# Last stage of a mixture-of-experts kernel in chunks of neighbouring tokens, with the residual added in the expert tiles

## What is computed

```python
gate_logits = jnp.einsum('bpd,de->bpe', x, W_gate)
top_w, top_idx = jax.lax.top_k(gate_logits, K)
top_w = jax.nn.softmax(top_w, axis=-1)
combine = jnp.einsum('bpke,bpk->bpe', jax.nn.one_hot(top_idx, E, dtype=x.dtype), top_w)
out = jnp.zeros_like(x)
for e in range(E):
    h = jax.nn.gelu(jnp.einsum('bpd,dm->bpm', x, W_in[e]) + b_in[e], approximate=False)
    y = jnp.einsum('bpm,md->bpd', h, W_out[e]) + b_out[e]
    out = out + combine[..., e, None] * y
...
x = _layernorm(x + _L1_ffn_ref(x, L1_ffn_W_gate, L1_ffn_W_in, L1_ffn_b_in, L1_ffn_W_out, L1_ffn_b_out), axis=-1)
```

## Time and profile before

| | |
|---|---|
| median of 3 runs | 1420.18 us (1419.89 to 1421.44) |
| profiled execution | 1420.47 us |
| its span | 1418.7 us |
| busy: TensorE / VectorE / ScalarE / GpSimd | 1246.8 / 959.8 / 657.1 / 470.6 us |
| first to last take_y of the expert stage | 1237.12 to 1379.46 us |
| last stage, first load issued to last output issued | 1382.91 to 1414.48 us |

### The profile page before, as it was taken

One profiled execution on the slowest core, in us unless ns is written; L12 is line 12 of the kernel. 1 busy time (PEld: TensorE's weight loads), 2 busy tenths in 40 slices (PEclk: granted clock), 3 DMA queues, 4 the chain that ended last, 5 costly groups with the idle time before them and its releaser, 6 DMA issues. The chain is left out here.

```text
span 1418.7 us, 45417 instructions
## 1 busy us (share of the span) xinstructions
PE 1246.8 (88%) x16752; PEld 764.3 (54%) x16753; DVE 959.8 (68%) x2010; ACT 657.1 (46%) x1313; POOL 470.6 (33%) x492
## 2 busy tenths in 40 slices
PE   6679999999999978999999999999999947399980
PEld 3235444444444433457465656566564626399980
DVE  6867888788877842275867667585858474466656
ACT  4146676666766664342425252433324221155553
POOL 7102211212112211042534334261615253254456
PEclk9589999999999998999999999999999978599995
DMA  6462211121121213030303030221303050322215
GB/s 193 123 203 59 52 46 53 54 61 48 48 61 52 57 33 104 28 75 24 102 22 102 0 109 15 68 56 39 91 8 90 14 150 9 107 69 63 67 55 178
DMA packets 96159, 98.87 MB, mean 70 GB/s; under 512 B 16032, under 2 KB 80416, under 8 KB 95904
## 3 DMA queue, kind: packets, MB, share of 16 engines
q1 hardware_dynamic: 82240, 81.21, 20.7%
q0 software_dynamic: 5216, 11.35, 2.5%
q10 hardware_dynamic: 8576, 4.46, 1.1%
HBM read 51.94 MB, written 24.72 MB: 54 GB/s over the span
## 5 line engine op out<-in xcount | busy, mean ns | idle before, releaser
L1451 DVE TENSOR_REDUCE arena<-banks 128x4 f32<-128x512 f32 (+3 forms) x336 | 343.6, 1067 | 82.1 <-PE banks L1231 77.3
L1388 ACT ACTIVATE arena<-banks 128x512 f32<-128x512 f32 x576 | 304.8, 605 | 184.9 <-PE banks L1231 179.9
L1231 PE MATMUL banks<-arena 99*32 99x512 bf16 (+7 forms) x6144 | 343.4, 335 | 29.0 <-ACT arena L1388 11.3
L1231 PEld LDWEIGHTS banks<-arena 96*32 96x32 bf16 (+1 forms) x6144 | 151.6, 97 | 195.9 <-ACT arena L1388 69.9
L433 PE MATMUL banks<-arena,h 128*128 128x512 f32 x512 | 226.7, 593 | 2.4 <-DVEq L378 1.0
L1573 POOL TENSOR_SCALAR_AFFINE_SELECT arena<-arena 128x512 f32<-128x512 f32 x128 | 79.6, 634 | 402.1 <-ACT arena L1388 401.3
L1298 PE MATMUL banks<-arena 128*32 128x512 f32 (+3 forms) x1536 | 153.3, 489 | 11.1 <-POOL arena L1573 10.9
L433 PEld LDWEIGHTS banks<-arena,h 128*128 128x128 f32 x512 | 94.8, 190 | 109.9 <-issue 104.4
L581 ACT ACTIVATE arena<-banks,sh 128x512 f32<-128x512 f32 x64 | 44.0, 687 | 217.9 <-PE banks L433 217.9
L449 POOL TENSOR_TENSOR arena<-arena 128x4 f32<-128x4 f32 x23 | 23.4, 1017 | 267.8 <-DVE arena L447 267.8
L962 ACT ACTIVATE arena<-banks,b_in 128x128 f32<-128x128 f32 x288 | 82.0, 368 | 62.4 <-PE banks L944 62.4
(11 more groups left out here) (171 smaller groups left out, 1768.9 us busy)
## 6 DMA issues: line engine op xcount, KB each, us to landing
arena<-arena SPq DMA_DIRECT2D x160, 128.0 KB, 2.7
arena<-k_parts SPq DMA_DIRECT2D x96, 96.0 KB
arena<-rows SPq DMA_DIRECT2D x72, 65.0 KB
arena<-q_parts SPq DMA_DIRECT2D x64, 64.0 KB
arena<-best SPq DMA_DIRECT2D x16, 256.0 KB, 4.5
k_parts<-arena SPq DMA_DIRECT2D x24, 128.0 KB, 3.1
arena<-q_parts SPq DMA_DIRECT2D x32, 96.0 KB
q_parts<-arena POOLq DMA_DIRECT2D x18, 128.0 KB, 3.0
```

Of the source, the lines that this page charges most:

```text
L1231: ins = nc.tensor.matmul(dst[c:c + 32, :], lhs[:, c:c + 32], rhs, start=start, stop=stop, skip_group_check=True)
L1388: nc.scalar.activation(pe_[:, s % NSLOT, :], score[s % NBANK], ACT.Exp, scale=SCALE0)\
L1451: nc.vector.tensor_reduce(mx[:, 1 if k0 else 0, qt, hs[0]:hs[-1] + 1], src, AX.X, ALU.max)\
```

## The change

The residual is no longer stored, reloaded and added at the end. Since the two weights of a token sum to 1, each expert tile adds its own rows times their weight, and the sum of the two results then holds the residual once. In the tile, VectorE's weigh becomes mix: x_g times weight plus the weighed bias, to y_g; take_y adds y_g to down's result times weight; the weighing of the bias goes to ScalarE, one tile ahead and in front of gelu. A new semaphore s_mix counts the mixes: weigh waits by it for its buffer.

In the last stage a chunk is half of one of the four sequences; a partition holds four neighbouring tokens, which are 2 KB in HBM. The loads come from two queues, SyncE's for the first and ScalarE's for the second result. The addition of the two is on VectorE, the negation of the mean on GpSimd, and SyncE issues the outputs; ScalarE's normalisations stand behind its eight loads.

```diff
@@ third layer norm
-            layernorm(tp, 3, "res3_1", res, x3, [("scatter7", 1), ("stored", 1)])
+            layernorm(tp, 3, "res3_1", res, x3, [("scatter7", 1)])
             tp.do("act", "x3_again", ["norm3", ("scatter7", 1)], lambda: nc.scalar.copy(x3_rows[:, 1, :, 0:C], x3))
-            tp.do("act", "stored", ["norm3"], lambda: nc.scalar.dma_start(
-                rest_d[bass.ds(c, 1)].rearrange("c p b k -> p (c b) k"), x3), line="out")
@@ views of the last stage
-        best_v = best[0:TOPK * NT, :].rearrange("(r b c p) k -> r c p b k", r=TOPK, b=B, p=P)
+        best_v = best[0:TOPK * NT, :].rearrange("(r b p h e) k -> r b h p e k", r=TOPK, b=B, p=P, h=2)
-        out_v = out.rearrange("b (c p) k -> c p b k", p=P)
+        out_v = out.rearrange("b (p h e) k -> b h p e k", p=P, h=2)
@@ expert tiles
             def take_y(J, k):
                 e.wait_ge(s_down, XG * J + k + 1)
+                e.wait_ge(s_mix, XG * J + k + 1)
+                nc.vector.scalar_tensor_tensor(out=y_g[:, k, :], in0=banks[:, 4 + k % 2, 0:P],
+                                               scalar=x_g[:, k, C + 1:C + 2], in1=y_g[:, k, :],
+                                               op0=ALU.mult, op1=ALU.add).then_inc(s_y, 1)
+
+            def mix(J, k):
                 e.wait_ge(s_bias, XG * J + k + 1)
                 wait(s_back[k], 16 * J)
-                nc.vector.scalar_tensor_tensor(out=y_g[:, k, :], in0=banks[:, 4 + k % 2, 0:P],
+                nc.vector.scalar_tensor_tensor(out=y_g[:, k, :], in0=x_g[:, k, 0:C],
                                                scalar=x_g[:, k, C + 1:C + 2], in1=bias[:, k % 2, :],
-                                               op0=ALU.mult, op1=ALU.add).then_inc(s_y, 1)
+                                               op0=ALU.mult, op1=ALU.add).then_inc(s_mix, 1)
 
             def weigh(J, k):
                 e.wait_ge(s_xg[k], 16 * (J + 1))
                 e.wait_ge(s_w1, XG * J + k + 1)
-                wait(s_y, XG * J + k - 1)
-                nc.vector.tensor_scalar(bias[:, k % 2, :], w_now[:, k % 4, 512:512 + C], x_g[:, k, C + 1:C + 2], None, ALU.mult).then_inc(s_bias, 1)
+                wait(s_mix, XG * J + k - 1)
+                nc.scalar.activation(bias[:, k % 2, :], w_now[:, k % 4, 512:512 + C], ACT.Copy,
+                                     scale=x_g[:, k, C + 1:C + 2]).then_inc(s_bias, 1)
@@ the steps of each engine
-            chain = {"sp": [(load, 0)], "pe": [(turn, 3), (up, 1), (down, 0)], "act": [(gelu, 0)],
-                     "dve": [(take_x, 3), (take_w, 2), (weigh, 1), (take_y, 0)], "pool": [(back, 0)]}[me]
+            chain = {"sp": [(load, 0)], "pe": [(turn, 3), (up, 1), (down, 0)], "act": [(weigh, 1), (gelu, 0)],
+                     "dve": [(take_x, 3), (take_w, 2), (mix, 0), (take_y, 0)], "pool": [(back, 0)]}[me]
-            if me == "sp":
-                for c in range(T // P):
-                    e.dma_start(parts[c][0], rest_d[c]).then_inc(s_rest, 16)
@@ last stage
-            if me == "sp":
+            if me in ("sp", "act"):
                 for k in range(XG):
                     e.wait_ge(s_back[k], 16 * NJ)
...
+                one, two = parts[c]
+                if me in ("sp", "act"):
+                    r = 0 if me == "sp" else 1
+                    e.dma_start((one, two)[r], best_v[r, c // 2, c % 2]).then_inc(s_parts[c], 16)
+                if me == "dve":
                     e.wait_ge(s_parts[c], 32)
-                    nc.gpsimd.tensor_tensor(one, one, two, ALU.add).then_inc(s_both, 1)
...
-                    nc.vector.tensor_tensor(total, total, one, ALU.add).then_inc(s_d, 1)
+                    nc.vector.tensor_tensor(one, one, two, ALU.add).then_inc(s_d, 1)
...
-                    nc.vector.tensor_scalar(less_e[:, c, :], mv_e[:, c, :, 0], -1.0, None, ALU.mult).then_inc(s_var4, 1)
...
+                    nc.gpsimd.tensor_scalar(less_e[:, c, :], mv_e[:, c, :, 0], -1.0, None, ALU.mult)\
+                        .then_inc(s_rstd4, 1)
...
-                    e.dma_start(out_v[c], one).then_inc(s_out, 16)
+                if me == "sp":
                     e.wait_ge(s_norm, c + 1)
+                    e.dma_start(out_v[c // 2, c % 2], two).then_inc(s_out, 16)
```

More of the change, by code:

```diff
@@ L126, in program @@
         best = nc.dram_tensor("best", [TOPK * NT + 2 * NE * P, C], F32, kind="Internal").ap()
-        rest_d = nc.dram_tensor("rest_d", [T // P, P, B, C], F32, kind="Internal").ap()
         att_t = nc.dram_tensor("att_t", [NU, HQ, D0, T], F32, kind="Internal").ap()
@@ L307, in program @@
         halves = [q_dec.rearrange("p a i b t -> p (a i b t)"), state.rearrange("p b i d -> p (b i d)"),
-                  sm.rearrange("p a t -> p (a t)"), hid[1].rearrange("p a t -> p (a t)")]
+                  sm.rearrange("p a t -> p (a t)"), o_t.rearrange("p b i t -> p (b i t)")]
         def quarter(x, k):
             return x[:, 512 * k:512 * k + 512].rearrange("p (b t) -> p b t", b=B)
-        parts = [(quarter(o_t.rearrange("p b i t -> p (b i t)"), k), quarter(halves[k // 4], k % 4),
-                  quarter(halves[2 + k // 4], k % 4)) for k in range(T // P)]
-        best_v = best[0:TOPK * NT, :].rearrange("(r b c p) k -> r c p b k", r=TOPK, b=B, p=P)
+        parts = [(quarter(halves[k // 4], k % 4), quarter(halves[2 + k // 4], k % 4)) for k in range(T // P)]
+        best_v = best[0:TOPK * NT, :].rearrange("(r b p h e) k -> r b h p e k", r=TOPK, b=B, p=P, h=2)
         s_experts = sem("s_experts")
@@ L908, in experts @@
                 e.wait_ge(s_pad, 16 * 2 * NE)
-            left = {"sp": [(s_line["scat"], 16 * TOPK * B * (NITER - 2))], "act": [(s_line["out"], 16 * NITER)]}
+            left = {"sp": [(s_line["scat"], 16 * TOPK * B * (NITER - 2))]}
             for s, v in left.get(me, []):
@@ L1027, in experts @@
             for c in range(NC):
-                total, one, two = parts[c]
-                if me == "sp":
-                    for r, dst in enumerate((one, two)):
-                        e.dma_start(dst, best_v[r, c]).then_inc(s_parts[c], 16)
-                if me == "pool":
-                    e.wait_ge(s_parts[c], 32)
-                    nc.gpsimd.tensor_tensor(one, one, two, ALU.add).then_inc(s_both, 1)
-                if me == "dve":
-                    if c == 0:
-                        e.wait_ge(s_rest, 16 * NC)
-                    e.wait_ge(s_both, c + 1)
-                    nc.vector.tensor_tensor(total, total, one, ALU.add).then_inc(s_d, 1)
-                    e.wait_ge(s_d, 3 * c + 1)
-                    for t in range(B):
-                        ins = nc.vector.bn_stats(st_e[:, c, t, 0:6], total[:, t, :])
+                one, two = parts[c]
@@ new lines, in experts @@
+                if me in ("sp", "act"):
+                    r = 0 if me == "sp" else 1
+                    e.dma_start((one, two)[r], best_v[r, c // 2, c % 2]).then_inc(s_parts[c], 16)
+                if me == "dve":
+                    e.wait_ge(s_parts[c], 32)
+                    nc.vector.tensor_tensor(one, one, two, ALU.add).then_inc(s_d, 1)
+                    e.wait_ge(s_d, 4 * c + 1)
+                    for t in range(4):
+                        ins = nc.vector.bn_stats(st_e[:, c, t, 0:6], one[:, t, :])
@@ L1043, in experts @@
                     ins.then_inc(s_d, 1)
-                    e.wait_ge(s_d, 3 * c + 2)
-                    for t in range(B):
+                    e.wait_ge(s_d, 4 * c + 2)
+                    for t in range(4):
                         ins = nc.vector.bn_aggr(mv_e[:, c, t, :], st_e[:, c, t, 0:6])
                     ins.then_inc(s_d, 1)
-                    e.wait_ge(s_d, 3 * c + 3)
-                    nc.vector.tensor_scalar(var_e[:, c, :], mv_e[:, c, :, 1], EPS, None, ALU.add).then_inc(s_var4, 1)
@@ L1050, in experts @@
-                    nc.vector.tensor_scalar(less_e[:, c, :], mv_e[:, c, :, 0], -1.0, None, ALU.mult).then_inc(s_var4, 1)
-                def scales(c):
-                    e.wait_ge(s_var4, 2 * c + 2)
+                    e.wait_ge(s_d, 4 * c + 3)
+                    nc.vector.tensor_scalar(var_e[:, c, :], mv_e[:, c, :, 1], EPS, None, ALU.add).then_inc(s_d, 1)
+                if me == "pool":
+                    e.wait_ge(s_d, 4 * c + 4)
                     nc.gpsimd.tensor_tensor(rstd_e[:, c, :], var_e[:, c, :], minus_half[:, :], ALU.pow)\
@@ L1054, in scales @@
                         .then_inc(s_rstd4, 1)
-                    e.wait_ge(s_rstd4, 2 * c + 1)
+                    nc.gpsimd.tensor_scalar(less_e[:, c, :], mv_e[:, c, :, 0], -1.0, None, ALU.mult)\
+                        .then_inc(s_rstd4, 1)
+                    e.wait_ge(s_rstd4, 3 * c + 2)
                     nc.gpsimd.tensor_tensor(less_e[:, c, :], less_e[:, c, :], rstd_e[:, c, :], ALU.mult)\
                         .then_inc(s_rstd4, 1)
-                if me == "pool":
-                    for k in ([c - 1] if c else []) + ([c] if c == NC - 1 else []):
-                        scales(k)
```

(8 more changed lines are left out.)

10 lines of the change are left out of this document (5 added, 5 removed).

## The result

| | before | after |
|---|---|---|
| median of 4 runs each | 1420.04 us | **1458.51 us** (1457.8 to 1458.94) |
| profiled execution | 1420.47 us | 1457.8 us |
| first to last take_y | 142.3 us | 187.1 us |
| last stage, first load issued to last output issued | 31.57 us | 24.45 us |

The change is slower by 2.7%: the ratio is 1.0273, with an interval from 1.0256 to 1.0291. The prediction was 1456 us, in a range from 1436 to 1471. Both parts of its sum have the expected sign: the expert stage is 44.7 us longer and the last stage 7.1 us shorter, +37.6 us together, where the two profiled executions are 37.3 us apart.

A forecast was written before the change was run, and what follows sets the result against it. TensorE was taken to bound the expert stage; the change adds a circle there, + 43 us, and shortens the last stage, - 7 us. From 1420.5 us profiled that gives 1456.3, forecast 1456 us, range 1436 to 1471.

The forecast's parts named there:

- The bound, and what to ask of it: Expert stage: TensorE bounds it, 142.3 us for 71 steps; nothing else must be faster, only how late each engine may get matters.
- The circle: Expert stage: down(k) depends on down(k-2) over VectorE and ScalarE, 5.35 us for two tiles, the stage 43 us longer.
- The weakest step: ScalarE, weigh to the first gelu: 0.88 us, taken from VectorE's register load, since no row shows one waited for on ScalarE.
- hidden load: Rival, 12%: ScalarE's sequencer has the expert's number already while waiting for mix; weigh to gelu 0.3 us, 1438 us in all.
- VectorE's rows don't agree with it: Argument against the sequencer reading on during a wait: take_y waits for down, yet take_w comes 0.88 us after take_x.
- The size of weigh: ScalarE, expert stage: one weigh activation a tile, estimated at 0.39 us from the skill's figures; no row showed this form.
- the held mix: Rival, 4%: GpSimd's scatter holds VectorE's mix, the circle 0.5 us longer, 1474 us; sign: a mix over 0.6 us.
- the falling clock: Rival, 5%: TensorE, no longer always busy, is granted 1.2 GHz for half the expert stage; about 1504 us.
- The faster case: Rival, 6%: ScalarE's weigh is never late, TensorE still bounds the expert stage, only the last stage's gain counts; 1413 us.
- TensorE idle some 0.7 us before each down group: Expected sign of the circle in the expert stage, with ScalarE releasing TensorE each time.
- These two balance: VectorE, expert stage: weigh removed (0.28 us a tile) and mix added (0.35 us) were said to balance.
- The reason for 3.3 us: Last stage: a chunk's two loads start together on two queues, so the first addition comes 3.0 to 3.74 us after first issue.

The follow-up runs named there:

- e3: The changed kernel with gelu's expert number loaded on ScalarE in weigh, ahead of weigh's waits; order and buffers stay: 1442.55 us, ratio 1.0135.
- e5: The changed kernel with weigh behind gelu on ScalarE and mix one tile ahead on VectorE: 1412.23 us, ratio 0.9949 to the kernel before.
- e1: The changed kernel with only weigh and gelu exchanged on ScalarE, gelu first: 1420.6 us, ratio 0.9983 to the kernel before.
- e6: e5 with the last stage's old views, tokens 1024 apart in runs of 512 bytes, still on two queues: 1413.44 us, ratio 0.9954.
- e8: e5 with all sixteen loads of the last stage issued by SyncE: 1412.45 us, ratio 0.9945.
- e9: Expert tiles of the kernel before with the changed last stage, the residual left out of the result: 1411.86 us, ratio 0.9945.
- e7: e5 with the addition of the two results back on GpSimd, ahead of the chunk before's power and products: 1414.43 us, ratio 0.9967.

## Why the prediction was right

**The bound, and what to ask of it** held. TensorE bounded the stage, and the question of how late each other engine may get found the circle before it had run. It was found in the order of instructions, not in busy times, which hardly changed.

**The circle** was summed as 5.35 us for two tiles and measured 5.29. Its links: take_x to take_w 0.84 (0.88), take_w to mix 0.48 (0.44), mix 0.34 (0.35), to ScalarE 0.10 (0.06), weigh to gelu 0.78 (0.88), the rest as predicted. First to last take_y was 185.5 us in the prediction and 187.1 in the trace, +44.7 for +43.

**The weakest step**, weigh to gelu, was taken from VectorE's register step at 0.88 us, between 0.3 and 1.1. The trace has 0.78 in the turn above. e3 shows both that the load is the step, and what a hidden load would give, 0.31. The gelus behind the table load without a hole spoke for the hidden load. They are weak evidence, as nothing between those two tiles had to wait and the load may have been done early; that is a reading and wasn't run. Nor do these runs tell what the sequencer does while only the instruction itself waits: the wait for s_mix is one of the sequencer's own, ahead of the activation, and take_y has more than one wait too. So "VectorE's rows don't agree with it" in the prediction said more than those rows show.

**The size of weigh** is 0.40 us. The Trainium skill, ScalarE: Activation LUTs, What ACT_TABLE_LOAD costs, gave an estimate of 0.39, and the trace agrees.

**The rivals.** The hidden load is refuted by 0.78 us, the held mix by 0.34 us beside GpSimd's scatters, the falling clock by a granted clock of 1.00 with TensorE busy 15.77 of 20 us, and in all seven windows from 1240 to 1380 us. The faster case is what e5 is, and it needed two steps moved.

**Where it missed.** Five steps, all small. "TensorE idle some 0.7 us before each down group" had the loss right and its form wrong: it is 1.2 us before every second one from the fourth pass on, since I had thought of one circle and not of two that run close together. The loop's 56 steps took 151.2 us and not 149.5: at the start of a pass a step is longer (2.43 us for 2.03), as in the kernel before (2.3 for 2.0), and I had counted all steps alike. "These two balance", of the weigh taken from VectorE and the mix put there, holds for the durations and not for the round: take_y waits for mix's end, so the pair takes 0.44 us; e1 shows the 5 us that this costs once the circle is gone. In the last stage the first addition came 4.11 us behind the first issue, outside my 3.0 to 3.74, the chunk took 2.12 us for 2.2, and the end 5.52 us for 5.7. These are + 0.8, - 0.6 and - 0.2 us and cancel, so 24.45 us for 24.4 is luck. The reason for 3.3 us, that two loads which start together land sooner than two that start 0.72 us apart, isn't what the rows show.

**What stays open** is why the first addition comes 4.1 us behind the first issue and came 3.74 before. The run's length alone and the number of queues alone don't do it, by e6 and e8; both together weren't run. In the profiles with the changed last stage it lies between 4.03 and 4.45 us (the longest in e9), and for the kernel before there is the one profile. Open too is how much of the 3.2 us that e7 leaves comes from the residual's addition alone.

## What to carry to other kernels

Where engines go through tiles in lists of steps, follow each new wait back through buffers and program order together until it meets the bounding engine again, a few tiles earlier; the sum of those links over the number of tiles is the pace, and busy time doesn't show it. A new step that nobody needs soon goes behind its engine's critical step and one tile further ahead of its reader: those two moves turned 1458.5 us into 1412.2. And a move to an engine with idle time is judged by its place in that engine's list, not by the idle time.

## What the runs showed of the hardware that I had not expected

- An instruction on VectorE that waits by a semaphore for the one in front of it, whose result it reads, starts about 0.1 us behind that one's end (mix at 1312.20 for 0.34 us, take_y at 1312.64 in e1), while independent ones overlap a little (0.31 us between starts for 0.34 us of length, in e5).
- GpSimd's power on 128 x 4 takes 1.03 us where VectorE has no addition of two SBUF inputs beside it (e7, and chunk 7 of the changed kernel) and 1.41 where it has. The Trainium skill, SBUF — State Buffer, Who interferes with whom, states that such instructions contend with a GpSimd instruction that reads SBUF; these rows agree. GpSimd's scatter from SBUF leaves VectorE's mix at 0.34 us, though that has two inputs from SBUF.
- The issue of a load of 256 KB takes 0.51 us in runs of 2 KB (0.53 with all on one queue, e8) and 0.89 in runs of 512 bytes on two queues (e6; 0.72 before, on one), while the first addition starts 4.07 us behind the first issue in the short runs and 4.03 to 4.45 us in the long ones.
